# Routing two mixture layers: seven of eight batches' logits computed inside the stage in front

## What is computed

```python
x = x + attention_L0(_layernorm(x), ctx, ...)
x = x + _L0_ffn_ref(_layernorm(x), gate_w, ...)   # softmax(xf @ gate_w), top 2 of 8, expert MLPs, final layernorm
x = x + attention_L1(...); x = x + ffn_L1(...)
x = x + window_attention_L2(ctx, _layernorm(x), ...)      # ends in tanh(cat @ W_c.T)
x = x + _L2_ffn_ref(_layernorm(x), router_w, ...) # top 2 of 8 of x @ router_w.T, expert MLPs
x = x + attention_L3(...); x = x + ffn_L3(...)
```

## Time and profile before

| quantity | value |
|---|---|
| median of 3 runs | 2277.5 us (2274.49 to 2277.8) |
| the profiled execution, device time | 2274.97 us |
| its span on the core | 2273.2 us |
| TensorE (PE) busy | 1962.6 us, 86% of the span |
| VectorE (DVE) busy | 1311.3 us, 58% |
| ScalarE (ACT) busy | 941.6 us, 41% |
| GpSimd (POOL) busy | 592.4 us, 26% |
| mean granted clock of TensorE | 0.921 of full |

### The profile page before, as it was taken

One profiled execution on the slowest core, in us unless ns is written; L12 is line 12 of the kernel. 1 busy time (PEld: TensorE's weight loads), 2 busy tenths in 40 slices (PEclk: granted clock), 3 DMA queues, 4 the chain that ended last, 5 costly groups with the idle time before them and its releaser, 6 DMA issues. The chain is left out here.

```text
span 2273.2 us, 37869 instructions
## 1 busy us (share of the span) xinstructions
PE 1962.6 (86%) x11930; PEld 1464.5 (64%) x11931; DVE 1311.3 (58%) x2977; ACT 941.6 (41%) x2050; POOL 592.4 (26%) x582
## 2 busy tenths in 40 slices
PE   6998669999758886999889739999999996997787
PEld 3665546666535553666566639999999983665455
DVE  5885656666468886787655262222222215887887
ACT  3545224444345543333222413333333323553787
POOL 1122346666434421011000032222222221321000
PEclk9999579999969998999988559999999997999899
DMA  7001211211141104000000611111111114100001
GB/s 269 1 1 63 71 58 60 65 60 62 50 159 62 50 1 162 0 0 0 2 15 3 241 33 33 37 37 37 37 35 35 37 33 158 38 20 1 10 28 38
DMA packets 71122, 119.54 MB, mean 53 GB/s; under 512 B 13648, under 2 KB 54736, under 8 KB 67952
## 3 DMA queue, kind: packets, MB, share of 16 engines
q1 hardware_dynamic: 55760, 78.76, 10.0%
q0 software_dynamic: 13680, 37.37, 5.2%
q10 hardware_dynamic: 1584, 2.13, 0.3%
HBM read 86.90 MB, written 31.33 MB: 52 GB/s over the span
## 5 line engine op out<-in xcount | busy, mean ns | idle before, releaser
L1427 ACT ACTIVATE e_hT<-psum,x_bt 128x128 f32<-128x128 f32 x568 | 154.6, 383 | 336.4 <-PE psum L1390 336.4
L1390 PEld LDWEIGHTS psum<-e_xT,e_w 128*128 128x128 f32 x2272 | 268.4, 194 | 8.4 <-ACT e_xT L1420 4.9
L1390 PE MATMUL psum<-e_xT,e_w 128*128 128x128 f32 x2272 | 269.1, 277 | 4.2 <-ACT e_xT L1420 4.2
L268 POOL TENSOR_TENSOR rstd<-lnt,half 128x4 f32<-128x4 f32 (+1 forms) x72 | 73.2, 1016 | 765.5 <-DVE lnt L262 765.5
L1399 PE MATMUL psum<-m_w,e_hT 128*128 x1136 | 256.8, 379 | 0.0
L1399 PEld LDWEIGHTS psum<-m_w,e_hT 128*128 128x128 f32 x1136 | 210.4, 190 | 25.7
L1448 DVE COPY e_w<-m_w 128x2048 f32 x71 | 87.1, 1227 | 227.0 <-PE psum L1390 225.7
L724 DVE TENSOR_REDUCE a_mx<-psum 128x8 f32<-128x512 f32 x192 | 123.2, 683 | 83.6 <-PE psum L515 83.0
L1247 ACT ACTIVATE e_hT<-psum,x_bt,x_gt 128x128 f32<-128x128 f32 x284 | 106.9, 457 | 142.8 <-PE psum L1214 142.8
L1331 POOL DMA_INDIRECT rows_out<-e_y,dst x106 | 105.6, 997 | 206.7 <-DVE e_y L1458 175.2
L1323 POOL DMA_INDIRECT e_x<-rows_in,src x142 | 141.9, 999 | 56.8 <-issue 35.2
(11 more groups left out here) (287 smaller groups left out, 3587.7 us busy)
## 6 DMA issues: line engine op xcount, KB each, us to landing
m_w<-in_L_ffn_w SPq DMA_DIRECT2D x16, 1024.0 KB, 9.2
m_w<-in_L_ffn_w SPq DMA_DIRECT2D x16, 512.0 KB, 12.3
m_w<-rows_out SPq DMA_DIRECT2D x16, 512.0 KB, 5.9
a_ar_g<-rows_out SPq DMA_DIRECT2D x16, 512.0 KB, 5.1
rows_in<-r_work SPq DMA_DIRECT2D x12, 512.0 KB, 5.8
x_res<-in_x SPq DMA_DIRECT2D x8, 512.0 KB, 6.9
m_w<-rows_in SPq DMA_DIRECT2D x8, 512.0 KB, 3.9
out_x<-x_res SPq DMA_DIRECT2D x8, 512.0 KB, 3.0
```

Of the source, the lines that this page charges most:

```text
L1390: mm = pe.matmul(h_b[s][:, f, :], w1[:, kk, f * P:(f + 1) * P], xT[s][:, kk, :], start=(kk == 0), stop=(kk == DC - 1))
L1427: g = act.activation(hT[s][:, f, :], h_b[s][:, f, :], ACT.Gelu, bias=bt[:, bass.ds(e * FC + f, 1)])
```

## The change

A new class `RouterFront` does the router's front for batches 0 to 6 (`AHEAD = 7`) inside the stage before: in a0 for layer 0, in w2 for layer 2. The dispatch does batch 7 alone. Per tile the same instructions run, in other pieces:

- in a0, ScalarE normalises one tile at the end of each tile's turn; TensorE transposes one tile (two transposes) into the free half of `out_b` right behind `project`, and `y_ps` is signalled after both; VectorE copies it out (`take_rows`, 128x256) ahead of the residual; the eight logit matmuls of a batch run in the free part of `pr_b` in front of `keys_values` or in its place; VectorE copies 128x32 logits out. GpSimd adds the post bias per batch, two of the seven after the last `root`;
- in w2, ScalarE normalises four tiles after the tanhs of a step, copies the transposed rows (two copies of 128x512 per batch) and the logits; TensorE runs logits and four transposes in front of the wait on `p_done`, and four transposes after the scores. The hardware loops of w2 are unrolled;
- the output norms of a0 and w2 also compute the shift on GpSimd (one more small instruction per batch);
- SP stores each normalised batch from these stages and waits at their end for all stores; in the dispatch all first-layer weights are issued at once, the expert constants after the second `select` has begun;
- `select` runs on 28 tiles at once at the start of the dispatch, and on 4 tiles when their logits are there. VectorE's wait for the stores is gone.

```diff
-        out_norm = Norm(k, sem, nm + "out")
+        router = RouterFront(k, sb, sem, nm + "r_", L, 2) if L == 0 else None
+        out_norm = Norm(k, sem, nm + "out", k.shift if router else None)
...
+                    if router:
+                        if b == 0:
+                            pool.wait_ge(router.post_in, 16)
+                        if b > 2:
+                            router.add_post(pool, b - 3)
                 out_norm.root(pool, NB - 1)
+                if router:
+                    for r in range(NB - 3, AHEAD):
+                        router.add_post(pool, r)
...
                     wait_pos(pe, drained, DRAINS * b)
+                    if router and b > 4:
+                        router.logits(pe, b - 5, pr_b[:, D:LG])
...
                         mm = pe.matmul(out_b[:, 0:D], oT[t // 2][:, c, t % 2, :], w["o"][:, c, :],
                                        start=(c == 0), stop=(c == DC - 1))
+                    if router and n >= TPB + 1:
+                        mm = router.turn(pe, n - TPB - 1, out_b[:, D:2 * D])
                     mm.then_inc(y_ps, 1)
...
+                        elif t == 3 and router:
+                            pe.wait_ge(drained, DRAINS * NB)
+                            router.logits(pe, b - 3, pr_b[:, D:LG])
...
+                    if router and t == 1:
+                        router.logits(pe, NB - 3, pr_b[:, D:LG])
+                if router:
+                    pe.wait_ge(x_added, NT)
+                    router.turn(pe, AHEAD * TPB - 1, out_b[:, D:2 * D]).then_inc(y_ps, 1)
+                    router.logits(pe, AHEAD - 1, pr_b[:, D:LG])
...
+                        if router and n >= 2 * TPB - 1:
+                            router.normalise(act, n - 2 * TPB + 1, out_norm.centred)
...
+                if router:
+                    for m in range(NT - 2 * TPB + 1, AHEAD * TPB):
+                        router.normalise(act, m, out_norm.centred)
...
+                def take_rows(m):
+                    dve.tensor_copy(router.zT[m // TPB % 2][:, :, m % TPB * P:(m % TPB + 1) * P],
+                                    out_b[:, D:2 * D].rearrange("p (c q) -> p c q", c=DC)).then_inc(router.copied, 1)
...
+                def take_logits(r):
+                    dve.wait_ge(router.lg_ps, r + 1)
+                    dve.tensor_copy(router.taken(r), pr_b[:, D:LG]).then_inc(router.lg_read, 1)
...
                 def residual(n):
                     dve.wait_ge(y_ps, n + 1)
+                    if router and n >= TPB + 1:
+                        take_rows(n - TPB - 1)
                     dve.tensor_tensor(k.xt(n), out_b[:, 0:D], k.xt(n), ALU.add).then_inc(x_added, 1)
...
                         if t == 0 and more:
                             drain_values(b + 1, 1 - s)
...
                     residual(NT - TPB + t)
                 out_norm.moments(dve, NB - 1)
...
+                    take_logits(NB - 3)
+                    dve.wait_ge(y_ps, NT + 1)
+                    take_rows(AHEAD * TPB - 1)
+                    take_logits(AHEAD - 1)
...
+                sp.wait_ge(z_done, 1)
+                sp.dma_start(k.zs[P + AHEAD * SEQ:P + NB * SEQ, :].rearrange("(t p) d -> p t d", p=P),
+                             z.rearrange("p (t d) -> p t d", t=TPB)).then_inc(stored, 16)
+                sp.wait_ge(selected, 2)
+                load_expert_constants(sp, k, L)
+                sp.wait_ge(stored, 16)
...
-                    for t in range(TPB):
-                        n = b * TPB + t
-                        o = act.activation(z[b % Z][:, t * D:(t + 1) * D], k.xt(n), ACT.Identity,
-                                           bias=shift[:, n:n + 1], scale=k.rstd[:, n:n + 1])
-                    o.then_inc(z_done, 1)
-                def copy(b, s):
-                    act.wait_ge(zT_ps, b + 1)
-                    wait_pos(act, lg_ps, b - 1)
-                    act.activation(zT[s][:, :, :], bank[s][:, :, :], ACT.Copy).then_inc(zT_copied, 1)
-                act.wait_ge(centred, 1)
-                normalise(0)
-                normalise(1)
-                for b in range(NB):
-                    copy(b, b % 2)
-                    if b + 2 < NB:
-                        normalise(b + 2)
+                for t in range(TPB):
+                    n = EARLY + t
+                    o = act.activation(z[:, t * D:(t + 1) * D], k.xt(n), ACT.Identity, bias=k.shift[:, n:n + 1],
+                                       scale=k.rstd[:, n:n + 1])
+                o.then_inc(z_done, 1)
+                act.wait_ge(zT_ps, 1)
+                act.activation(zT[:, :, :], bank[:, :, :], ACT.Copy).then_inc(zT_copied, 1)
...
-                    dve.wait_ge(lg_ps, (h + 1) * (HALF // TPB))
+                def select(tiles):
...
-                    dve.tensor_copy(src, lg[h][:, 0:HALF * E].rearrange("p (t e) -> p t e", t=HALF)
-                                    ).then_inc(lg_read, 1)
-                    dve.wait_ge(lg_read, h + 1)
+                    bc = lambda t: t.to_broadcast([P, tiles.stop - tiles.start, E])
...
-                for h in range(2):
-                    select(h)
+                select(slice(0, EARLY))
+                dve.wait_ge(lg_ps, 1)
+                dve.tensor_copy(lgt[:, EARLY:NT, :], lg[:, 0:TPB * E].rearrange("p (t e) -> p t e", t=TPB)
+                                ).then_inc(lg_read, 1)
+                dve.wait_ge(lg_read, 1)
+                select(slice(EARLY, NT))
...
                 dve.wait_ge(place_ps, 1)
-                for s in range(Z):
-                    dve.wait_ge(stored[s], 16 * NB // Z)
...
+    def normalise(self, act, m, centred):
+        k, r, t = self.k, m // TPB, m % TPB
+        if t == 0:
+            act.wait_ge(centred, r + 1)
+            if r > 1:
+                act.wait_ge(self.copied, TPB * (r - 1))
+                act.wait_ge(self.stored[r % 2], 16 * (r // 2))
+        act.activation(self.z[r % 2][:, t, :], k.xt(m), ACT.Identity, bias=k.shift[:, m:m + 1],
+                       scale=k.rstd[:, m:m + 1]).then_inc(self.z_done, 1)
+    def turn(self, pe, m, dst):
+        pe.wait_ge(self.z_done, m + 1)
+        for c in range(DC):
+            mm = pe.transpose(dst[:, c * P:(c + 1) * P], self.z[m // TPB % 2][:, m % TPB, c * P:(c + 1) * P], self.k.ident)
+        return mm
+    def logits(self, pe, r, dst):
+        pe.wait_ge(self.gate_in, 16)
+        pe.wait_ge(self.copied, TPB * (r + 1))
+        wait_pos(pe, self.lg_read, r)
+        zT = self.zT[r % len(self.zT)]
+        for t in range(TPB):
+            for c in range(DC):
+                mm = pe.matmul(dst[:, t * E:(t + 1) * E], zT[:, c, t * P:(t + 1) * P], self.k.gate[:, c, :],
+                               start=(c == 0), stop=(c == DC - 1))
+        mm.then_inc(self.lg_ps, 1)
...
+    def taken(self, r):
+        return self.k.lgt[:, r * TPB * E:(r + 1) * TPB * E]
...
+    def add_post(self, pool, r):
+        k = self.k
+        pool.wait_ge(self.z_done, TPB * (r + 1))
+        xs = k.x[:, r * (TPB * D):(r + 1) * (TPB * D)].rearrange("p (t d) -> p t d", t=TPB)
+        pool.tensor_tensor(xs, xs, self.post_b[:, None, :].to_broadcast([P, TPB, D]), ALU.add)
...
+AHEAD = NB - 1
...
+                    if b > 2:
+                        router.store(sp, b - 3)
+                for r in range(NB - 3, AHEAD):
+                    router.store(sp, r)
+                router.all_stored(sp)
...
+                def take_rows(r, half):
+                    act.wait_ge(r_ps, 2 * r + half + 1)
+                    to = router.zT[0][:, :, half * 2 * P:(half + 1) * 2 * P].rearrange("p c (t q) -> p t c q", t=2)
+                    act.activation(to, rb[:, :].rearrange("p (t c q) -> p t c q", t=2, c=DC),
+                                   ACT.Copy).then_inc(router.copied, 2)
+                def take_logits(r):
+                    act.wait_ge(router.lg_ps, r + 1)
+                    act.activation(router.taken(r), tb[:, D:LG], ACT.Copy).then_inc(router.lg_read, 1)
...
+                    if b > 1:
+                        take_rows(b - 2, 0)
                     act.wait_ge(t_ps, b + 1)
                     act.activation(pT[:, :], tb[:, 0:TPB // 2 * P], ACT.Copy).then_inc(t_copied, 1)
+                    if b > 2:
+                        take_logits(b - 3)
+                    if b > 1:
+                        take_rows(b - 2, 1)
                     wait_pos(act, x_added, b - 1)
                     for t in range(TPB):
                         m = b * TPB + t
                         act.wait_ge(y_ps, m + 1)
                         act.activation(th[s][:, t, :], yb[t % 2][:, 0:D], ACT.Tanh).then_inc(t_done, 1)
+                    if b > 0:
+                        for t in range(TPB):
+                            router.normalise(act, (b - 1) * TPB + t, norm.centred)
...
+                take_logits(NB - 3)
+                for half in range(2):
+                    take_rows(AHEAD - 1, half)
```

(16 more changed lines are left out.)

148 lines of the change are left out of this document (80 added, 68 removed).

## The result

| | before | changed |
|---|---|---|
| median of the runs | 2277.65 us (2274.49 to 2279.98, 4 runs) | 2243.76 us (2239.4 to 2244.14, 4 runs) |
| profiled execution | 2274.97 us, span 2273.2 | 2244.04 us, span 2242.2 |
| TensorE busy | 1962.6 us, 86% | 1940.1 us, 87% |
| VectorE busy | 1311.3 us, 58% | 1318.4 us, 59% |
| ScalarE busy | 941.6 us, 41% | 935.3 us, 42% |

The ratio is 0.9847, with a 95% interval of 0.9831 to 0.9862: 34 us faster, where 16.5 was forecast. The direction was right. The size was that of the second case (2244), to which the prediction gave 15%. Here "the clock" is TensorE's granted clock, 1.00 or 0.50 of full, and work at 0.50 is called cold.

The account below looks back on a forecast made before the run. It took TensorE to bound the dispatch fronts (mostly at 1.2 GHz), a0 and w2. -32.4 - 35.0 + 25.4 + 26.9 = -15.1 from the profiled 2274.97 gave 2259.9, forecast as a median of 2261 us, range 2242 to 2280.

Parts of the forecast that it names:

- second case: Rival, 15%: the clock holds, as added work fills the last w2 batch's idle time and the falls don't come; 2244 us.
- Dispatches, -32.4 and -35.0: Layers 0 and 2: batch 7's front alone costs 9.2 us, replacing 40.2 and 42.8; the second `select` saves 1.4 each.
- a0, +25.4: a0 grows by turns inside steps 5.4, logits of five batches 9.5, serial tail 8.8 and clock 1.7 us.
- the two additions: End of a0: two GpSimd bias additions, 2 x 2.36 = 4.7 us, with nothing beside them.
- w2, +26.9: w2 grows by steps 12.0, step 2 2.7, last batch 2.7, tail 2.5 and clock falls 7.0 us.
- one such fall of 3.5 us per batch with logits: Four w2 steps: each logits block lowers TensorE's clock for 3.5 us, half of it lost, 7.0 us in all.
- I keep it cold: Last batch of w2: clock stays at 0.50; logits cost 3.4 us, less 0.7 to 1 filling idle time: +2.7.
- the step, 3.0 forecast: Each of four w2 steps gains eight logit matmuls, 1.9, and twice four transposes, 0.55: 3.0 us, 12.0 together.
- ScalarE's four normalises: Step 2 of w2: normalises (2.1 us) delay the exponentials TensorE's transposes await; with 0.6 for turns, +2.7.
- The tail: w2 after the last tanh: normalises, copies and cold logits take 7.3 us where 4.87 stood, +2.5.
- third case: Rival, 20%: w2 falls to 1.2 GHz and stays; 2304 us if in all four steps, 2279 if in half.
- The fourth: Rival, 15%: in a0 VectorE's copy delays TensorE 0.4 us per tile, 11 us in all; 2271 us.

Follow-up runs that it names:

- run 5: The change with a quarter of the logit matmuls in a0 (only each batch's first tile), against the change: a0 227.2 us, one profiled run.
- Run 4: The change with the logit matmuls in steps 3 to 7 of w2 issued twice: 2263.42 us, w2 153.3, one profiled run.
- Runs 2: The change with the last w2 step's logits and first four transposes moved behind the softmax wait: 2254.95 us, w2 145.1 instead of 132.7.
- run 3: The kernel before with 16 useless transposes in TensorE's wait in the last step of w2: 2269.59 us, ratio 0.9961, w2 118.5 instead of 124.6.
- tails_and_warm: The change with reordered tails of a0 and w2, plus useless 128x512 matmuls at the starts of a1 (20), w2 (6), a3 (7 and 10): 2245.53 us.
- run 6: The change with one more VectorE operation of 0.4 us before each copy in a0: a0 240.0 us, one profiled run.
- run 8: The change again, 2239.87 us; with reordered tails, 2235.5; those plus useless matmuls in TensorE's waits, 2245.53, or fewer (12 in a1, none in w2), 2233.6.

## Why the prediction was wrong

- **Dispatches, -32.4 and -35.0: right**, -32.3 and -35.0; front 8.9 us for 9.2, everything behind it hidden. One reason in it was wrong: it read the 3.42 us of x16 as sixteen matmuls, two batches' worth, and took the whole for one batch because of slow weight loads. The x16 are the eight matmuls of one batch at the low clock, and measured 3.58.
- **a0, +25.4: near**, +29.0. Other profiles of it have a0 at 239.9 to 243.9 and the old one at 214.3 to 216.1, so 25.4 lies among them. It has three parts.
  - 3.6 us ahead of the second batch's queries, which are no term of the change. There the clock rises early or late by the execution, for good at 29.4 us in the profile of before, at 39.4 in this one and at 30.2 in run 5's, whose code is the same up to there: the second batch's queries begin between 41.2 and 42.8 us in the three profiles with the old a0, and between 41.9 and 45.3 with the new one.
  - From there to the last batch's queries 145.4 for 134.0: +11.4, with turns at 0.66 a batch (0.9 taken), logits 1.8 (1.9) in three batches and two falls of 1.6 (one of 1.7).
  - The rest, +13.9, are two more batches' logits (3.6), turns (1.3) and 9.0 of tail (8.8 taken). In the tail the price of the two additions was right, but not that nothing runs beside them: TensorE's and VectorE's chain ended 1.7 us before them.
- **w2, +26.9: wrong**, +8.1. The term that failed first is "one such fall of 3.5 us per batch with logits ... 4 x 1.75 = 7.0". It measured 0: the block as the change has it, amid the 128x256 matmuls of w2, didn't lower the clock once in four steps. The rows that it rested on the earlier trace rows were of the dispatch and of a1, whose surroundings differ. Run 4 shows that such falls exist with twice the matmuls; the profiles of a0 show one or two for the five blocks in its steps and tail. So its size was wrong for w2, not its kind.
- The second is "I keep it cold", the last batch at +2.7. It measured -3.7 (from 17.0 us between the last-but-one batch's end and the last tanh's end to 13.4). The prediction had counted the 2.73 us of idle time, let the moved work fill 0.7 to 1 of it, and kept the clock where it was; that the fill could hold the clock stood in its second case alone. The moved work takes 2.4 us there, and 1.50 of wait remain. Runs 2 and 3 show from both sides that this wait made the long fall: opening it costs w2 12.4 us, filling it in the kernel before gives 6.1. That the wait left over cost only a short fall was favourable: in `tails_and_warm` the same wait cost a long one.
- The third is the step, 3.0 forecast and 1.72 measured, 5.1 over the four: 0.9 each for small waits now filled, 0.4 for transposes and logits faster back to back than their rows. ScalarE's four normalises cost step 2 1.3 instead of 2.7. The tail was +3.5 for +2.5.
- 7.0 + 6.4 + 5.1 + 1.4 - 1.0 = 18.9 of the 18.8 us between the forecast and w2.
- **The cases.** The second case's first reason, the filled wait, was right. Its 2244 was met in part by luck: its terms give w2 +11.7 and a0 +23.7, and they measured +8.1 and +29.0. Its second reason, that the falls don't come, held in the steps of w2 and not in a0, where two came; and as a rule that a busy TensorE keeps its clock whatever it does, run 4 refutes it. The third case didn't come; even in run 4 each fall ended again, at 153.3 us of w2. The fourth is refuted by run 6.

What stays open: how much of such matmuls next to how much other work lowers the clock. The runs show two amounts in w2 (16 records: none; 32: four falls) and two in a0 (16: one or two falls in five batches; 4: none). And open is what decides whether a fall behind a short wait lasts 3.4 us or the rest of the stage.

## What to carry to other kernels

Before pricing added work, ask what it does to the clock of the work behind it: a wait of TensorE of 2.7 to 3.9 us in front of a long stretch cost more here through the lower clock than through itself, and work put into it, even of no use, paid for itself where it ended inside the wait (run 3, a1 in run 8) and not where a wait was left open behind it (a3). Added work can also lower the clock with no wait at all, as the eight-column matmuls of run 4 did; an experiment with twice of it shows how near that is. A term that rests on a row from another stage should carry the range of both ends, and a wait that the same paragraph fills should not be kept in the sum.

## What the runs showed of the hardware

- Sixteen transposes of no use in a wait of 2.73 us took 6.1 us off a stage (clock 1.00 for 0.50 over the last batch; run 3).
- With TensorE busy in each of 20.50 us, the granted clock was 0.50 for 10.20 of them, where 32 records of eight-column matmuls stood in a step; with 16 it was 1.00 throughout (run 4).
- The same wait of 1.5 us in front of the same work was followed by 3.4 us at 0.50 in five profiles and by the whole rest of the stage at 0.50 in one (run 8).
- The same code takes longer where less clock is granted: the kernel before took 2271 to 2285 us over 39 runs, at mean clocks of 0.925 and 0.917 at the two ends, and the experts of layer 0, the same code in all profiles, 325.2 us at 0.978 and 330.2 at 0.955.
